# Four PSUM banks for the scores, one for the pieces: a re-ordered attention layer in an eight-layer kernel

## The reference

```
xn = _layernorm(x, gamma, beta)          # of an x that was itself normalised first
q = (xn @ w_q).reshape(B, SQ, 16, 64)
k, v = split(context @ w_kv)             # each reshaped to 16 heads of 64
scores = einsum('bqhd,bkhd->bhqk', q * 64 ** -0.5, k)
attn = softmax(scores, axis=-1)
out = einsum('bhqk,bkhd->bqhd', attn, v).reshape(B, SQ, 1024) @ w_out + b_out
x = x + tanh(g_xattn[3]) * out * tanh(gate[0])
```

## Time and profile before

| what | value |
| --- | --- |
| runs (3) | 1843.51, 1844.87, 1848.87 us; median 1844.87 |
| span of the profiled execution | 1861.1 us; its own device time is not among the runs listed |
| mean granted TensorE clock | 0.886 of full speed |
| busy, share of the span | PE 75%, DVE 72%, ACT 55%, POOL 26% |
| stage A3 | from 948 us (first transpose) to 1480 us (last projection) |
| chunks 0 to 7 of A3, scores to scores | 54.3, 60.3, 63.0, 65.3, 65.3, 62.4, 60.0 us, and 57.6 to the last but two values |

### The profile page before, as it was taken

The page is one execution under the profiler, slowest core; times in us unless marked ns, Lnnn a source line. Parts: engine busy times, 40 slices in busy tenths (PEclk is TensorE's granted clock), DMA queues, the critical chain, the costliest instruction groups (busy, mean ns, idle before and its releaser), DMA issues.

```text
span 1861.1 us, 35910 instructions
## 1 busy us (share of the span) xinstructions
PE 1404.8 (75%) x9844; PEld 1054.7 (57%) x9844; DVE 1333.1 (72%) x4156; ACT 1024.2 (55%) x2876; POOL 492.1 (26%) x499
## 2 busy tenths in 40 slices
PE   3677776987734446676769998989997409999995
PEld 3455554665523334433325666666666408999995
DVE  3888886888879986889945667766766455666665
ACT  3677785432425553311037777767785326777773
POOL 5433530221100001100000032232233333555451
PEclk9999998999965557978789999999999758999998
DMA  7000069300199910000000000000000052222226
GB/s 167 7 7 6 12 83 160 48 0 1 34 145 157 162 18 17 28 1 0 1 6 1 7 26 22 16 29 23 10 23 24 27 223 61 64 66 68 64 64 227
DMA packets 144711, 97.75 MB, mean 53 GB/s; under 512 B 21658, under 2 KB 133934, under 8 KB 143443
## 3 DMA queue, kind: packets, MB, share of 16 engines
q1 hardware_dynamic: 135890, 79.49, 23.2%
q0 software_dynamic: 8704, 16.87, 2.8%
HBM read 42.43 MB, written 54.93 MB: 52 GB/s over the span
## 4 chain that ended last, share of the span: by engine, by line
PE 36%; issue 31%; DVE 17%; ACT 9%; POOL 2%; DMA 1%; SPq 1%; another core or an unknown queue 1%; DVEq 1%; ACTq 0%; POOLq 0%
PE bank L1227 6%; PE bank L1219 6%; PE bank L863 5%; PE bank L912 3%; PE bank L879 3%; ACT att L1383 2%; ACT arena L1260 2%; PE bank L899 2%; PE bank L889 2%; DVE nm L1699 2%; PE bank L867 2%; DVE att L1700 1%; DVE tmp L1977 1%; DVE arena L1843 1%
## 5 line engine op out<-in xcount | busy, mean ns | idle before, releaser
L1260 ACT ACTIVATE arena<-bank 128x512 f32<-128x512 f32 (+6 forms) x440 | 255.5, 614 | 141.2 <-PE bank L1083 61.5
L540 POOL TENSOR_TENSOR rstd<-ve,mhalf 128x4 f32<-128x4 f32 x64 | 67.0, 1046 | 688.2 <-DVE ve L1680 688.2
L1383 ACT ACTIVATE att<-bank,arena 128x128 f32<-128x128 f32 x512 | 181.5, 377 | 81.8 <-DVE arena L1843 79.9
L1615 ACT ACTIVATE att<-bank,arena 128x128 f32<-128x128 f32 x576 | 164.6, 371 | 69.9 <-PE bank L1219 67.6
L639 POOL DMA_INDIRECT dispatched_rows<-arena x128 | 132.5, 1035 | 222.0 <-DVE arena L1761 153.5
L690 POOL DMA_INDIRECT expert_outputs<-arena x144 | 144.7, 1005 | 148.1 <-issue 102.9
L1260 ACT ACTIVATE xnT<-bank 128x128 f32<-128x128 f32 (+1 forms) x180 | 63.4, 352 | 190.2 <-PE bank L711 134.8
L1227 PE MATMUL bank<-arena,att 128*128 128x128 f32 x1152 | 154.1, 277 | 3.0 <-ACT att L1615 1.9
L1219 PE MATMUL bank<-xnT,arena 128*128 128x128 f32 x1152 | 154.1, 277 | 0.2 <-ACT xnT L1260 0.2
L1227 PEld LDWEIGHTS bank<-arena,att 128*128 128x128 f32 x1152 | 141.0, 193 | 5.3 <-ACT att L1615 5.3
L1219 PEld LDWEIGHTS bank<-xnT,arena 128*128 128x128 f32 x1152 | 141.6, 194 | 0.8 <-ACT xnT L1260 0.8
(11 more groups left out here) (324 smaller groups left out, 3306.1 us busy)
## 6 DMA issues: line engine op xcount, KB each, us to landing
dispatched_rows<-padf SPq DMA_DIRECT2D x16, 2128.5 KB, 35.4
arena<-dispatched_rows SPq DMA_DIRECT2D x144, 64.5 KB
cxT<-in_ctx SPq DMA_DIRECT2D x32, 256.0 KB, 2.7
arena<-in_L_ffn_w SPq DMA_DIRECT2D x8, 1024.0 KB
arena<-expert_outputs SPq DMA_DIRECT2D x8, 1024.0 KB, 13.7
expert_outputs<-arena POOLq DMA_INDIRECT x144
dispatched_rows<-arena POOLq DMA_INDIRECT x128
out_x<-x SPq DMA_DIRECT2D x8, 256.0 KB, 4.8
```

Source lines behind the costliest of these rows:

```text
L1260: copy = lambda o, i: nc.scalar.activation(o, i, ACT.Copy)
L1383: last = nc.scalar.activation(ex3_of(w, side)[:, i, :], bank[side][:, i * P:i * P + P], ACT.Exp, bias=nm3[:, w % 2, h:h + 1], accum_out=su ...
L1615: last = nc.scalar.activation(h3[:, s % 2, k * P:k * P + P], bank[s % 2][:, k * P:k * P + P], ACT.Gelu, bias=b1c3[:, s % 4, k:k + 1])
```

## The change

The scores get four banks: step w writes banks 0 and 1 when w is even, 2 and 3 when it is odd, so that they wait for the exponentials of step w-2 only. The transposed probabilities of both sides go through bank 4, one side after the other, each waiting until ACT has copied the side before. The values go to bank 5. All pieces go through bank 6, so each waits until the one just before it has been copied. Projections keep bank 7.

The orders within a step are new:

- PE: scores(w), p0, probs_T(w-1) side 0, values(w-2), probs_T(w-1) side 1, p1, project (even w), p2 (p3), routing.
- ACT: p0, probs_T(w-1) side 0, exponentials side 0, p1, probs_T(w-1) side 1, exponentials side 1, p2 (p3), routing.
- DVE: normal(w-1, side 1), maxima(w), residual or routing or front, values(w-2), normal(w, side 0).

No instruction of arithmetic is added or removed. The diff:

```diff
--- before.py
+++ after.py
@@ -143,7 +143,10 @@
             return bank[(6 - s) % 8] if first else bank[6]
 
         def slice_bank3(p, s, first):
-            return bank[(6 - s) % 8] if first else bank[6 - (p + s) % 2]
+            return bank[(6 - s) % 8] if first else bank[6]
+
+        def score_bank(w, side):
+            return bank[w % 2 * 2 + side]
 
 
         x = sb("x", [P, B, P])
@@ -846,7 +849,7 @@
                 def piece(c, p, s, first=False):
                     A = slice_bank3(p, s, first)
                     if not first:
-                        pe.wait_ge(sem("A3_slice_gone"), c * SLICES3 + s)
+                        pe.wait_ge(sem("A3_slice_gone"), c * SLICES3 + (s + 1))
                     elif s >= 8:
                         pe.wait_ge(sem("A3_slice_gone"), s - 6)
                     if s == 0:
@@ -869,25 +872,24 @@
 
                 def scores(c, p, w):
                     j, half = divmod(w, 2)
-                    reach(pe, "A3_exp", c, 2 * PAIRS, 2 * w)
+                    reach(pe, "A3_exp", c, 2 * PAIRS, 2 * (w - 1))
                     if w == 0:
                         pe.wait_ge(sem("A3_slices_ready"), c + 1)
                     for i in range(HQ):
                         for side in range(2):
                             r = slice(D3 * side, D3 * side + D3)
                             q, k = (qk3[r, p, t + half * HQ + i, j * P:j * P + P] for t in (0, HEADS // 2))
-                            last = nc.tensor.matmul(bank[side][:, i * P:i * P + P], q, k, start=True, stop=True)
+                            last = nc.tensor.matmul(score_bank(w, side)[:, i * P:i * P + P], q, k, start=True, stop=True)
                             if i == HQ - 1:
                                 last.then_inc(sem("A3_scores"), 1)
 
-                def probs_T(c, w):
-
-                    for side in range(2):
-                        pe.wait_ge(sem("A3_normal"), c * (2 * PAIRS) + (2 * w + side + 1))
-                        reach(pe, "A3_pT", c, 2 * PAIRS, 2 * (w - 1) + side + 1)
-                        for i in range(HQ):
-                            last = nc.tensor.transpose(bank[2 + side][:, i * P:i * P + P], ex3_of(w, side)[:, i, :], ident[:, :])
-                        last.then_inc(sem("A3_pT_full"), 1)
+                def probs_T(c, w, side):
+
+                    pe.wait_ge(sem("A3_normal"), c * (2 * PAIRS) + (2 * w + side + 1))
+                    reach(pe, "A3_pT", c, 2 * PAIRS, 2 * w + side)
+                    for i in range(HQ):
+                        last = nc.tensor.transpose(bank[4][:, i * P:i * P + P], ex3_of(w, side)[:, i, :], ident[:, :])
+                    last.then_inc(sem("A3_pT_full"), 1)
 
                 def values(c, p, w):
 
@@ -896,7 +898,7 @@
                     reach(pe, "A3_oT", c, PAIRS, w)
                     for i in range(HQ):
                         for side in range(2):
-                            last = nc.tensor.matmul(bank[4][D3 * side:D3 * side + D3, i * P:i * P + P], v3[p][:, j, 2 * HQ * half + 2 * i + side, :],
+                            last = nc.tensor.matmul(bank[5][D3 * side:D3 * side + D3, i * P:i * P + P], v3[p][:, j, 2 * HQ * half + 2 * i + side, :],
                                                     pT3(w, side)[:, i, :], start=True, stop=True)
                     last.then_inc(sem("A3_pv"), 1)
 
@@ -919,17 +921,22 @@
                         mine = slices3_at(w) if more else []
                         if live:
                             scores(c, p, w)
+                        for s in mine[:1]:
+                            piece(c + 1, 1 - p, s)
+                        before = (live and w >= 1) or (not first and w < 1)
+                        if before:
+                            probs_T(c if w else c - 1, (w - 1) % PAIRS, 0)
+                        if (live and w >= 2) or (not first and w < 2):
+                            values(c, p if w >= 2 else 1 - p, w - 2)
+                        if before:
+                            probs_T(c if w else c - 1, (w - 1) % PAIRS, 1)
+                        for s in mine[1:2]:
+                            piece(c + 1, 1 - p, s)
                         if w % 2 == 0 and (live and w >= 4):
                             project(c, (w - 4) // 2)
                         if w % 2 == 0 and (not first and w < 4):
                             project(c - 1, (w - 4) % PAIRS // 2)
-                        for s in mine[:1]:
-                            piece(c + 1, 1 - p, s)
-                        if (live and w >= 1) or (not first and w < 1):
-                            probs_T(c, w - 1)
-                        if (live and w >= 2) or (not first and w < 2):
-                            values(c, p if w >= 2 else 1 - p, w - 2)
-                        for s in mine[1:]:
+                        for s in mine[2:]:
                             piece(c + 1, 1 - p, s)
                         if live and not first and w in (3, 4, 6):
                             routing(c - 1, {3: 8, 4: 9, 6: 12}[w])
@@ -1380,28 +1387,28 @@
                     reach(act, "A3_normal", c, 2 * PAIRS, 2 * (w - 2) + side + 1)
                     for i in range(HQ):
                         h = 2 * i + side
-                        last = nc.scalar.activation(ex3_of(w, side)[:, i, :], bank[side][:, i * P:i * P + P], ACT.Exp,
+                        last = nc.scalar.activation(ex3_of(w, side)[:, i, :], score_bank(w, side)[:, i * P:i * P + P], ACT.Exp,
                                                     bias=nm3[:, w % 2, h:h + 1], accum_out=sums3[:, w % 2, h:h + 1])
                     last.then_inc(sem("A3_exp"), 1)
 
                 def probs_T(c, w, side):
                     act.wait_ge(sem("A3_pT_full"), c * (2 * PAIRS) + (2 * w + side + 1))
                     reach(act, "A3_pv", c, PAIRS, w - 1)
-                    copy(pT3(w, side), b4(2 + side)).then_inc(sem("A3_pT"), 1)
+                    copy(pT3(w, side), b4(4)).then_inc(sem("A3_pT"), 1)
 
                 def body(c, p, more, first=False, live=True):
                     for w in range(PAIRS if live else DRAIN3):
                         mine = slices3_at(w) if more else []
+                        before = (live and w >= 1) or (not first and w < 1)
                         for side in range(2):
+                            for s in mine[side:side + 1]:
+                                piece(c + 1, 1 - p, s)
+                            if before:
+                                probs_T(c if w else c - 1, (w - 1) % PAIRS, side)
                             if live:
                                 exponentials(c, w, side)
-                            for s in mine[side:side + 1]:
-                                piece(c + 1, 1 - p, s)
-                        for side in range(2):
-                            if (live and w >= 1) or (not first and w < 1):
-                                probs_T(c, w - 1, side)
-                            for s in mine[2 + side:3 + side]:
-                                piece(c + 1, 1 - p, s)
+                        for s in mine[2:]:
+                            piece(c + 1, 1 - p, s)
                         if live and not first and w in (3, 5, 6):
                             routing(c - 1, {3: 8, 5: 9, 6: 10}[w])
 
@@ -1840,7 +1847,7 @@
                 def maxima(c, w):
                     for side in range(2):
                         dve.wait_ge(sem("A3_scores"), c * (2 * PAIRS) + (2 * w + side + 1))
-                        v.tensor_reduce(nm3[:, w % 2, side:2 * HQ:2], b4(side), AX, ALU.max, negate=True).then_inc(sem("A3_max"), 1)
+                        v.tensor_reduce(nm3[:, w % 2, side:2 * HQ:2], b4(w % 2 * 2 + side), AX, ALU.max, negate=True).then_inc(sem("A3_max"), 1)
 
                 def normal(c, w, side):
 
@@ -1854,7 +1861,7 @@
                     dve.wait_ge(sem("A3_pv"), c * PAIRS + (w + 1))
                     if half == 0:
                         reach(dve, "A3_y", c, CB, w // 2 - 1)
-                    v.tensor_copy(oT3[:, j % 2, HQ * half:HQ * half + HQ, :], b4(4)).then_inc(sem("A3_oT"), 1)
+                    v.tensor_copy(oT3[:, j % 2, HQ * half:HQ * half + HQ, :], b4(5)).then_inc(sem("A3_oT"), 1)
 
                 def front(c, k):
                     if k == 0:
@@ -1875,9 +1882,10 @@
 
                 def body(c, p, more, first=False, live=True, ahead=True):
                     for w in range(PAIRS if live else DRAIN3):
+                        if (live and w >= 1) or (not first and w < 1):
+                            normal(c if w else c - 1, (w - 1) % PAIRS, 1)
                         if live:
                             maxima(c, w)
-                            normal(c, w, 0)
                         if w == 2 and not first:
                             residual(c - 1)
                         if live and not first:
@@ -1888,7 +1896,7 @@
                         if (live and w >= 2) or (not first and w < 2):
```

(2 more changed lines are left out.)

## The result

The changed kernel is slower, 2.1%:

| | before | after |
| --- | --- | --- |
| median | 1846.87 us (1843.51 to 1849.28, 4 runs) | 1885.21 us (1883.66 to 1889.49, 4 runs) |
| ratio | | 1.021, interval 1.019 to 1.023 |
| profiled execution | span 1861.1, and 1845.2 in a second one (experiment 1) | span 1882.8 |

The account below looks back on a forecast made before the run. PE bounds chunks that make pieces, a chain of waits chunk 7. Chunks 1 to 6 +33, chunk 0 +5, chunk 7 -11 sum to +27: 1888 on the span, 1872 us on the median, range 1846 to 1892.

Parts of the forecast that it names:

- (a): Chunks 1 to 6: PE's projection waits for DVE's values and ACT's routing copy, and the chunk-end wait, go: 22.2 us.
- (b): One bank for pieces, chunks 1 to 6: new PE waits, mostly for ACT's copies, 6.7 us per chunk.
- (c): DVE's residual in step 2 waits for the moved projection, so PE waits 2.5 us once in each chunk.
- (d): Chunk 0: 7.2 us of new waits, against a vanished closing wait and a shorter step 0, net +5 us.
- (e): Chunk 7, without pieces: four score banks shorten its chain of waits from 57.6 to about 46.5 us, -11 (-4 to -14).
- drain: The drain's three steps keep their chain: 0, between -2 and +2 us.
- the clock: Rival: a PE wait of 2.5 us in each chunk brings half speed, 10.5 us more over seven chunks, 1883; chance 0.20.
- faster: Rival: ACT copies pieces while PE does other work, new waits under 28 us in chunks 1 to 6, 1818; chance 0.08.
- Residual hidden: Rival: DVE and ACT catch up before PE asks, so 6 x 2.5 us of waits go, 1857; chance 0.13.
- third and fourth score bank: Score banks in chunks 1 to 6: worth nothing, as no profile row shows a wait for them.

Follow-up runs that it names:

- experiment 1: The kernel before, profiled once more with no edit: 1846.97 us, span 1845.2.
- experiment 3: Changed kernel with scores rotating through three banks and pieces alternating between two: 1858.39 us, ratio 1.0051 to the kernel before.
- experiment 2: Changed kernel with DVE's residual and routing statistics of step 2 moved behind the values and first normalisation: 1873.23 us, ratio 1.0127 to before.
- experiment 4: Changed kernel with the edits of experiment 2 and experiment 3 together: 1843.01 us, ratio 0.9973 to the kernel before.
- experiment 5: Kernel of experiment 4 with scores back in banks 0 and 1, waiting for all exponentials of the step before: 1914.4 us, ratio 1.0220 to before.

## Why the prediction was right, and where its sum was off

It forecast slower, by two mechanisms, and both are shown: experiment 3 takes one away (27 us), experiment 2 the other (12), experiment 4 both (42 of 38). By its own terms, against the second profile of before (idle is the length of a stretch less PE's busy time in it, which leaves out the wait that ends chunk 0):

| term | forecast | measured |
| --- | --- | --- |
| (a) waits that go | 22.2 | 21.3, all of PE's idle time (366.6 - 345.3) |
| (b), (c) new waits, chunks 1 to 6 | 55 | 47.0, all of PE's idle time (400.1 - 353.1) |
| PE busier, chunks 1 to 6 | 0 | 7.8 (353.1 - 345.3) |
| chunks 1 to 6, net | +33 | +33.5 |
| (d) chunk 0 | +5 | +8.0 |
| (e) chunk 7 and drain | -11 | -5.1 |
| sum | +27 | +36.4, and 1.2 elsewhere |

**How the waits compare.** The forecast counted from start to start, the lists of waits count from the recorded end of a group, which lies later than the moment at which PE could start the next. So the 0.77 of the forecast and the 0.69 of the list are one and the same wait (1.71 measured from p1 to p2, 1.72 forecast). The same step in the second profile of before, to set beside 1056.15 to 1058.92 above:

```profile
1045.81 1.98 PE L863 MATMUL bank<-xnT,wqk 128*128 128x512 f32 x4
1047.72 1.16 PE L879 MATMUL bank<-arena 64*128 64x128 f32 x16
```

From p1 to the next scores it is 2.77 after and 1.91 before: 0.86 more, of which the list shows 0.69. The rest stands as busy time of PE. That explains most of the 7.8: in the five chunks with a granted clock of 1.00 the changed kernel has PE busy for 58.3 each, where before has 57.2 at the same clock, so 1.1 a chunk, 6.5 in six, come with the waits and with transposes in two groups instead of one, and not with the clock. In the prediction's own measure the new waits are thus 53.5 (47.0 + 6.5), 8.9 a chunk against 9.2. (c) was 2.5 and is 2.4: from p0 of step 3 to the transpose 3.37 (1067.93 to 1071.30) for 0.96, though DVE stands 4.26 and not 5.

Experiment 3 shows in addition that part of (b) was a wait beside another: it removes 21 us of piece waits, and 12 return at other places, behind ACT.

**What was luck.** The waits were counted 1.5 too high (55 for 53.5) and those that go 0.9 too high. The sum of (a) is right with other parts than I gave: projections wait 12.5 in the second profile and not 15.7, and a wait of 2.2 without a releaser and one of 1.5 for the transposed x fill the gap. And a rival of the prediction came true in a small part, the clock. After the wait of 2.25 us at 1206.07 the values took 1.57 where they take 1.09, and after one of 2.68 the scores took 1.89 where they take 1.16. Timeline of PE, changed kernel, chunk 3:

```profile
1176.17 1.89 PE L882 MATMUL bank<-arena 64*128 64x128 f32 x16 [2.68 <-issue]
...
1206.07 0.66 PE L891 MATMUL bank<-ident,att 128*128 128x128 f32 x4 [2.25 <-DVE att L1856]
1206.66 1.57 PE L901 MATMUL bank<-arena 128*64 128x128 f32 x16
```

Yet after 2.24 at 1071.30 in chunk 1 they took 1.09, and that chunk's granted clock is 1.00 as before, so it is not every wait of that length. Before the change it was not either: the 1.80 that the prediction called the longest in rows 3 isn't (1.9 stands there), and behind 1.95 at 1227.35 a piece took 1.12, full speed. Chunk 3, with 61.5 us busy at a granted clock of 0.95, is the only one of the six with such places, 3.2 us of them; the second profile of before has 1.9 of its own (chunk 5, 58.8 at 0.97, and a little in chunk 3). So the clock adds 1.3 us in chunks 1 to 6, where the rival's price was 10.5 for seven chunks.

(d): chunk 0 took +8.0 where I had +5. PE is idle there for 8.7 and was for 3.6, so 5.1 more; it is also busier by 2.9 (53.56 against 50.67), partly the ends of groups before new waits as above, partly half speed (granted clock 0.95 against 0.97). Two pieces at half speed there, PE, changed kernel:

```profile
985.05 1.90 PE L866 MATMUL bank<-xnT,wqk 128*128 128x512 f32 x2 [0.92 <-ACT arena L1375]
...
987.63 2.08 PE L866 MATMUL bank<-xnT,wqk 128*128 128x512 f32 x2 [0.69 <-ACT arena L1375]
```

(e) is **the term that was off most**, -5.1 with the drain for -11, less by its mechanism than by its base. From the first maxima to the last but two values the prediction had 45.4 us (43.3 + 2.1); DVE's timeline of the changed kernel gives 46.5:

```profile
1444.79 1.29 DVE L1850 TENSOR_REDUCE arena<-bank 128x4 f32<-128x512 f32 x2 [1.82 <-PE bank L882]
...
1491.33 0.68 DVE L1864 COPY arena<-bank 128x512 f32<-128x512 f32 x1
```

But the 57.6 from which I subtracted held some 4 us that the second profile doesn't have: in the second the same stretch runs from 1400.1 to 1453.8, 53.7. And the maxima did not start 1.1 us earlier; the scores ahead of them ran at half speed (2.08 for 1.16). So the chunk goes from 53.7 to 49.3, -4.4. The drain kept its chain within 1 us against the second profile (11.1 to 10.4); against the first it would have been 7 us shorter, without any part of the change. I took the span of 1861.1 to be 16 us above the median by a constant that leaves differences alone; some 10 of those us lay in the stretch of (e) and its drain.

With (e) and the drain 6 too low, (d) 3 too low and 1.2 elsewhere, the forecast of +27 came out 11 under the measured 38. These larger errors all point one way, so the nearness of the number owes nothing to them.

The rival *faster* fell at the point named: new waits came to 47 by the list, not under 28, though ACT did run ahead (its 79.9 of waiting for maxima fell to 1.7). *Residual hidden* fell by experiment 2. My statement that the third and fourth score bank are worth nothing in chunks 1 to 6 was argued from the order before, and holds there as far as its rows show; in the new order experiment 5 puts 46 us on the third, 24 of them as waits in those chunks (58.6 against 34.9 on one chip). The fourth is worth less than a second bank for pieces: experiment 3 moves it there and gains.

## What to carry to other kernels

Give the banks to the engine that sets the time: here ACT got them and its idle time only moved, while PE, busy 95% of a chunk, lost the second bank that hid a copy. How many banks a stage needs depends on the order: in the order before no row showed the scores waiting for a third bank, in the new one they need it. For each bank with one writer and one reader, write start to copy (1.06), copy (0.60) and release (0.06) beside the slot (0.96): where two such groups follow each other, one bank costs the difference every time. If banks rotate, the number of groups in the loop must come out right at its seam as well, and when a piece of filler work is moved later, look for who takes its result in the order of another engine. Before a term is read off one stretch of one profile, profile the kernel a second time.

## What was not expected of the hardware

Two profiled executions of one program differed by 16 us in span (1861.1 and 1845.2), with chunks 0 and 1 equal, 10 us more in chunks 2 to 6 and 10 in the last, in part as idle time that no engine of the program ends (the 2.12 of the earlier trace rows is of that kind, and absent in the second). Three chips ran the kernel before in 1848.5, 1873.9 and 1865.6 us, a spread of 1.4%, while the ratio of the changed kernel to it was 1.0210 on one and 1.0236 on another. Both differences have one shape. The changed kernel took 66.33 and 66.35 us in chunk 1 on two chips, but 333.8 and 355.6 in chunks 2 to 6; kernel 4 took 62.59 and 62.60, then 310.1 and 316.5; the first and second profile of before 60.31 and 60.30, then 316.0 and 306.3. POOL's sends of the routed rows begin at the end of chunk 1: in the changed kernel POOL is busy for 4.2 us in chunk 1 and for 17 to 20 in each of chunks 2 to 6. So the first profile may simply be from a slower chip; whether it is, and whether the sends are what differs, no run shows. What decides whether PE runs at half speed behind a wait of 2.2 us stays open too.
